# In 21 of 256 Mamba units ScalarE makes the product with B, with time on the partitions, and TensorE turns it into PSUM

## What is computed

```
rn = resid * rsqrt(mean(resid^2) + EPS) * norm_w
skip = rn @ skip_w.T
x_in = rn @ in_w.T
x = silu(conv(x_in))                    # causal, 4 taps, along time
delta = softplus(x @ wd1.T @ wd2.T + wd2_b)
Bm = x @ wB.T ;  Cm = x @ wC.T          # (L, 16) each
def step(h, (d_l, b_l, c_l, x_l)):      # h: (B, E, N)
    h = exp(d_l[:, :, None] * A) * h + (d_l * x_l)[:, :, None] * b_l[:, None, :]
    y_l = einsum('ben,bn->be', h, c_l)
y = (ys + x * W_D) * silu(skip)
return resid + y @ out_w.T
```

## Time and profile before

| | us |
|---|---|
| median of three runs | 1861.87 (1861.37 to 1863.11) |
| the profiled execution, its own time | 1862.27 |
| its span in the trace | 1860.5 |
| the Mamba layer in that span | 0 to about 912 |
| first scan to last scan | about 42 to 905 |
| granted TensorE clock, mean over the span | 0.976 |

### The profile page before, as it was taken

One profiled execution on the slowest core, in us unless ns is written; L12 is line 12 of the kernel. 1 busy time (PEld: TensorE's weight loads), 2 busy tenths in 40 slices (PEclk: granted clock), 3 DMA queues, 4 the chain that ended last, 5 costly groups with the idle time before them and its releaser, 6 DMA issues. The chain is left out here.

```text
span 1860.5 us, 26382 instructions
## 1 busy us (share of the span) xinstructions
PE 1704.0 (92%) x9245; PEld 1340.8 (72%) x9245; DVE 1474.0 (79%) x2310; ACT 1074.6 (58%) x1871; POOL 1100.2 (59%) x711
## 2 busy tenths in 40 slices
PE   6887989899898989966889999999999899999999
PEld 2455656565666666655778888888888788888888
DVE  4889999999999999999787777776345676666664
ACT  5867787878778787777534444443443444444442
POOL 2879999999999999999852222220454432222220
PEclk9899999999999999978999999999999999999999
DMA  6223333232333233344011111121000011111111
GB/s 200 83 77 98 102 98 102 87 113 92 107 96 99 93 107 99 96 150 140 7 35 35 35 35 35 35 57 23 7 0 0 1 46 45 44 38 46 46 46 46
DMA packets 113918, 125.63 MB, mean 68 GB/s; under 512 B 18816, under 2 KB 66048, under 8 KB 113664
## 3 DMA queue, kind: packets, MB, share of 16 engines
q1 hardware_dynamic: 113792, 124.03, 22.9%
HBM read 95.14 MB, written 4.72 MB: 54 GB/s over the span
## 5 line engine op out<-in xcount | busy, mean ns | idle before, releaser
L383 POOL TENSOR_TENSOR m_U<-m_U,m_C 128x1024 f32<-128x1024 f32 x255 | 601.0, 2369 | 26.0 <-DVE m_U L890 15.8
L525 PEld LDWEIGHTS m_y<-ident,m_U 128*128 128x128 f32 x2048 | 249.9, 147 | 117.8 <-issue 71.1
L890 DVE TENSOR_TENSOR_SCAN m_U<-m_dA,m_carry,m_U 128x512 f32<-128x512 f32 x256 | 310.5, 1262 | 4.9 <-ACT m_dA L758 4.5
L525 PE MATMUL m_y<-ident,m_U 128*128 128x128 f32 x2048 | 282.5, 284 | 29.4 <-POOL m_U L383 29.2
L890 DVE TENSOR_TENSOR_SCAN m_U<-m_dA,m_U 128x512 f32<-128x512 f32 x256 | 295.9, 1203 | 11.8 <-ACT m_dA L758 8.4
L758 ACT ACTIVATE m_dA<-high,m_negA 128x512 f32<-128x512 f32 x256 | 172.4, 685 | 74.2 <-DVE m_U L890 73.8
L758 ACT ACTIVATE m_dA<-even,m_negA 128x512 f32<-128x512 f32 x256 | 170.8, 684 | 56.6 <-DVE m_U L890 55.5
L1164 POOL TENSOR_TENSOR SW<-g_Rt 128x512 f32<-128x512 f32 x32 | 40.3, 1290 | 251.5 <-DMA g_CT<-SW 236.7
L1164 POOL TENSOR_TENSOR SW<-f_Rt 128x512 f32<-128x512 f32 x32 | 41.0, 1312 | 226.3 <-DMA f_CT<-SW 225.1
L506 PE MATMUL m_psB<-m_stack,m_pick 128*128 128x512 f32 x196 | 100.7, 514 | 34.1 <-DVE m_U L873 33.9
L873 DVE TENSOR_TENSOR m_U<-even,m_psB 128x1024 f32<-128x1024 f32 x100 | 119.6, 1196 | 12.0 <-PE m_psB L506 11.8
(11 more groups left out here) (389 smaller groups left out, 4414.6 us busy)
## 6 DMA issues: line engine op xcount, KB each, us to landing
m_C<-bc_rows SPq DMA_DIRECT2D x256, 256.0 KB, 3.2
m_B<-bc_rows SPq DMA_DIRECT2D x60, 256.0 KB, 3.5
f_CT<-SW SPq DMA_DIRECT2D x128, 64.0 KB, 2.1
g_CT<-SW SPq DMA_DIRECT2D x128, 64.0 KB, 2.1
even<-in_ffn_w SPq DMA_DIRECT2D x16, 256.0 KB, 5.2
f_z_raw<-f_turned_z SPq DMA_DIRECT2D x112, 32.0 KB, 1.9
g_z_raw<-g_turned_z SPq DMA_DIRECT2D x112, 32.0 KB, 1.9
out<-res SPq DMA_DIRECT2D x7, 512.0 KB, 2.8
```

What stands on the lines that cost most here:

```text
L383: pool.tensor_tensor(u, u, C[:, M % C_RING, :].unsqueeze(1).to_broadcast([P, PE_E, CHUNK]), ALU.mult).then_inc(hc_ready, 1)
L525: last = nc.tensor.matmul(y[:, t, j * P:(j + 1) * P], U[:, M % U_RING, j, t * P:(t + 1) * P], ident[:, :], start=False, stop=n == N - 1, i ...
L890: nc.vector.tensor_tensor_scan(u, dA[:, s % A_RING, :], u, carry[:, e, n:n + 1] if q else 0.0, ALU.mult, ALU.add).then_inc(scan_done, 1)
```

## The change

In chunks 1 to 7 three units in each (5, 10 and 19 of the chunk) are **turned**: 21 in all. For such a unit neither `spread_B` nor VectorE's or GpSimd's product is made. In their place:

- ScalarE holds `dxT` (dx with time on the partitions, four tiles of 128 steps) and `BT` (B the same way). `product(M)` multiplies, with B as the scale of each partition, in four instructions of 128x256 into the unit's place of the U ring, two steps ahead.
- TensorE's `turn_product(M + 1, j)` turns the four 128x128 blocks of each channel block into the PSUM bank of the dA ring that the decay would have had: j = 0 ahead of the parts of its step, j = 1 behind them.
- ScalarE writes the two decays of that unit to an SBUF tile `dAT`, and the scan takes the decay from there and the product from PSUM.
- For `dxT` and `BT` each chunk has new parts: `tr0` to `tr3` and `bt`, four transposes on TensorE and one copy on ScalarE each. `tr2` stands at unit 6, `tr3` at 9 (ScalarE: 10), `tr0` at 28, `tr1` and `bt` at 31.
- The 60 units of GpSimd stay 60, at other places: (3, 7, 12, 14) in the first half of chunks 1 to 7, (6, 9, 12, 15) in the second half of odd chunks, (6, 10, 13) in that of even ones. So VectorE makes 175 products in place of 196.
- To make room in SBUF the ring of C goes from eight tiles to three and that of B from two to one, loaded two units ahead. Two copies of feed-forward weights move from units 21 and 26 of the last chunk to 26 and 28.

The diff, cut to its core:

```diff
-    U_RING, C_RING, A_RING, B_RING = 6, 8, 3, 2
-    ON_POOL, AHEAD = ((3, 7, 10, 14), (4, 9, 14), (3, 7, 11, 14), (3, 6, 10, 14)), 3
+    U_RING, C_RING, A_RING = 6, 3, 3
+    ON_POOL, AHEAD, B_AHEAD = [((3, 7, 10, 14), (4, 9, 14))] + [((3, 7, 12, 14), (6, 9, 12, 15)), ((3, 7, 12, 14), (6, 10, 13))] * 4, 3, 2
+    TURNED, TURN_AHEAD = [((), ())] + [((5, 10), (3,))] * (CHUNKS - 1), 2
...
-                 5: ("cv1", "back3"), 6: ("cv1+",), 7: ("in2",), 8: ("cv2",), 9: ("cv2+",), 10: ("in3",),
+                 5: ("cv1", "back3"), 6: ("cv1+", "tr2"), 7: ("in2",), 8: ("cv2",), 9: ("cv2+", "tr3"), 10: ("in3",),
...
-                 27: ("out1",), 28: ("out1+",), 29: ("back0",), 30: ("back1",),
+                 27: ("out1",), 28: ("out1+", "tr0"), 29: ("back0",), 30: ("back1",), 31: ("tr1", "bt"),
...
-                if M in pool_units:
-                    i = BEFORE[M]
-                    need(sp, pool_mult, i - B_RING + 1)
-                    sp.dma_start(B[:, i % B_RING, :],
-                                 bc_rows[q, n:n + 1, :].to_broadcast([P, CHUNK])).then_inc(B_ready[i % B_RING], 16)
+                if M + B_AHEAD in pool_units:
+                    n_b = place(M + B_AHEAD)[3]
+                    assert n_b >= B_AHEAD
+                    need(sp, pool_mult, POOL_BEFORE[M + B_AHEAD])
+                    sp.dma_start(B[:, :], bc_rows[q, n_b:n_b + 1, :].to_broadcast([P, CHUNK])).then_inc(B_ready, 16)
...
+            def turn_product(M, j):
+
+                s = PE_E * M + j
+                pe.wait_ge(UT_ready, TURNED_BEFORE[M] + 1)
+                pe.wait_ge(scan_done, s - A_RING + 1)
+                for t in range(TILES):
+                    last = nc.tensor.transpose(dA[:, s % A_RING, t * P:(t + 1) * P],
+                                               U[:, M % U_RING, j, t * P:(t + 1) * P], ident[:, :])
+                last.then_inc(UT_turned, 1)
...
-                if M + 2 < ALL_UNITS and M + 2 not in pool_units:
+                if M + 2 in dve_units:
                     spread_B(M + 2)
+                if M + 1 in turned_units:
+                    turn_product(M + 1, 0)
                 for name, k in parts_of(PE_AT, M):
                     part(name, k)
+                if M + 1 in turned_units:
+                    turn_product(M + 1, 1)
...
-                nc.scalar.activation(dA[:, s % A_RING, :], delta[q][:, e, :], ACT.Exp,
+                to = dAT[:, s % PE_E, :] if s // PE_E in turned_units else dA[:, s % A_RING, :]
+                nc.scalar.activation(to, delta[q][:, e, :], ACT.Exp,
                                      scale=negA[:, e, n:n + 1]).then_inc(dA_ready, 1)
+
+            def product(M):
+
+                c, q, p, n = place(M)
+                for e in range(PE_E * p, PE_E * (p + 1)):
+                    wait_freed(act, f"tr{e}", c)
+                wait_freed(act, "bt", c)
+                act.wait_ge(nsum_done, M - U_RING + 1)
+                for t in range(TILES):
+                    last = nc.scalar.activation(U[:, M % U_RING, :, t * P:(t + 1) * P], dxT[:, pair(p), t, :], ACT.Copy,
+                                                scale=BT[:, t, n:n + 1])
+                last.then_inc(UT_ready, 1)
...
+                if M + TURN_AHEAD in turned_units:
+                    product(M + TURN_AHEAD)
...
+                decay, product = dA[:, s % A_RING, :], u
+                if M in turned_units:
+                    dve.wait_ge(UT_turned, PE_E * TURNED_BEFORE[M] + j + 1)
+                    decay, product = dAT[:, j, :], dA[:, s % A_RING, :]
```

More of the change, by code:

```diff
@@ L151, in mamba @@
         B_full, rows_ready, rows_out = sem("B_full"), sem("rows_ready"), sem("rows_out")
[L152 removed]
+        B_ready, pool_mult = sem("B_ready"), sem("pool_mult")
+        UT_ready, UT_turned = sem("UT_ready"), sem("UT_turned")
         C_ready = [sem(f"C_ready{i}") for i in range(C_RING)]
@@ L191, in mamba @@
         BEHIND = {"out0": -1, "out0+": -1, "out1": -1, "out1+": -1, "gate1": -1, "back2": -1, "back3": -1,
-                  "gate0": 0, "back0": 0, "back1": 0, "silu_g": 0, "sum": 2, "square": 2, "factors": 2, "norm": 2, "double": 2}
+                  "gate0": 0, "tr2": 0, "tr3": 0, "back0": 0, "back1": 0, "silu_g": 0, "sum": 2, "square": 2, "factors": 2, "norm": 2, "double": 2}
         ASKED = dict(enumerate((4, 1, 5, 0), CHUNKS))
@@ L199, in parts_of @@
             late = [(name, k) for slot, name, k in at["late"] if c == CHUNKS - 1 and slot == i]
-            chunks = [(name, k) for name, k in chunks if 0 <= k < CHUNKS and (name, k) != ("back1", CHUNKS - 1)]
+            chunks = [(name, k) for name, k in chunks if 0 <= k < CHUNKS and (name, k) != ("back1", CHUNKS - 1)
+                      and (k > 0 or name[:2] != "tr")]
             return chunks + late
@@ L239, in place, with before @@
             return c, c % 2, i // N, i % N
-        pool_units = [M for M in range(ALL_UNITS) if M % N in ON_POOL[M // N % (2 * PASSES)]]
-        BEFORE = [len([m for m in pool_units if m < M]) for M in range(ALL_UNITS)]
+        pool_units = [M for M in range(ALL_UNITS) if M % N in ON_POOL[M // UNITS][M // N % PASSES]]
+        turned_units = [M for M in range(ALL_UNITS) if M % N in TURNED[M // UNITS][M // N % PASSES]]
+        dve_units = [M for M in range(ALL_UNITS) if M not in pool_units and M not in turned_units]
+        def before(units):
+            return [len([m for m in units if m < M]) for M in range(ALL_UNITS + 1)]
+        POOL_BEFORE, TURNED_BEFORE, DVE_BEFORE = before(pool_units), before(turned_units), before(dve_units)
         def pair(p):
@@ L443, in part @@
                     last = mm(take(name, k), [(rnT[:, d, t:t + P], skw[:, d, :]) for d in range(KD)])
+                elif name[:2] == "tr":
+                    e = int(name[2])
+                    pe.wait_ge(dx_ready, KE * k + e + 1)
+                    out = take(name, k)
+                    for t in range(TILES):
+                        last = nc.tensor.transpose(out[:, t * P:(t + 1) * P], dx[q][:, e, t * P:(t + 1) * P],
+                                                   ident[:, :])
+                elif name == "bt":
+                    pe.wait_ge(rows_ready, k + 1)
+                    out = take(name, k)
+                    for t in range(TILES):
+                        last = nc.tensor.transpose(out[:, t * 2 * N:(t + 1) * 2 * N], rows[:, t * P:(t + 1) * P],
+                                                   ident[0:2 * N, 0:2 * N])
                 elif name[:2] == "cv":
@@ L889, in scan @@
                 dve.wait_ge(dA_ready, s + 1)
-                nc.vector.tensor_tensor_scan(u, dA[:, s % A_RING, :], u, carry[:, e, n:n + 1] if q else 0.0,
+                nc.vector.tensor_tensor_scan(u, decay, product, carry[:, e, n:n + 1] if q else 0.0,
                                              ALU.mult, ALU.add).then_inc(scan_done, 1)
@@ L908, in _ @@
             for M in range(ALL_UNITS):
-                if M + 1 < ALL_UNITS and M + 1 not in pool_units:
+                if M + 1 in dve_units:
                     mult(M + 1)
```

47 lines of the change are left out of this document (29 added, 18 removed), and 4 rows, old and new, of the table ACT_AT.

## The result

The changed kernel takes **1878.16 us** (median; 1876.83 to 1883.15), the kernel before 1861.91 (1860.7 to 1863.11): ratio 1.0091, 95% interval 1.0081 to 1.0101. It is 16.2 us slower. The forecast was 1860.6, the range ended at 1870: the prediction was wrong, by size and by sign. The profiled execution took 1877.32 us (span 1875.6).

The account below looks back on a forecast made before the run. The prediction took GpSimd to bound even chunks and VectorE odd ones. Chunks 1 to 4 gave +1.4, 5 and 6 -2.0, 7 -0.7: -1.3 on the profiled 1862.3, with the median 0.4 lower: 1860.6 us; range 1849 to 1870.

Parts of the forecast that it names:

- What bounds the kernel: Whole stretch: GpSimd sets even chunks, VectorE odd ones; a lighter VectorE can give at most GpSimd's 19.7 us of waits.
- VectorE, ScalarE, TensorE, DMA as single terms: VectorE 23.3 us less; per chunk ScalarE 81.8 to 89.4, TensorE 96.0 to 99.8 of 106; C's loads hidden.
- First half of an odd chunk: Walk from unit 5 to unit 10: waits sum to 2.3 us against 2 x 1.11 saved, net +0.1; wait bounds 1.0 and 3.5.
- Second half: Odd chunk: GpSimd's fourth product adds 2.33 us, less 0.6 won and waits of 0.7 and 0.4 swallowed, net +0.6.
- Even chunks: Set by GpSimd, with 0.4 us of waits in chunk 2; VectorE's lead grows there but cannot be used.
- Slower, TensorE paces the first half: TensorE's 22.8 us in steps 3 to 9 exceed VectorE's 21.0; 1.4 us in each of six chunks, 1870 us; chance 0.18.
- Faster: VectorE's lead from even chunks lasts through odd first halves, GpSimd pacing throughout; 1849 to 1856 us, middle 1853; chance 0.36.
- C's lateness: Rows of C land later than 4.7 us, at chunk starts or in chunk 7; 8 us more, 1870; chance 0.07.
- transposes that don't overlap: TensorE's 44 transposes cost 0.272 us each, 12.0 a chunk, filling it to 107 of 106; 1869 us; chance 0.02.

Follow-up runs that it names:

- r16: Changed kernel with each block of a turned unit turned twice into the same slot, 8 transposes where there were 4: 1893.53 us.
- r10: Changed kernel with dx's third quarter turned in step 7, behind the next input product, instead of step 6: 1874.44 us.
- r17: Kernel before with the changed kernel's smaller rings, B's fetch and later weight copies; no turned unit, no parts, old places of GpSimd's products: 1860.55 us.
- r4: Changed kernel with only the second halves' unit turned and GpSimd's new places there; first halves as in the kernel before: 1868.99 us.
- r9: Changed kernel with GpSimd's products of second halves at 5, 8, 11, 14 and 5, 9, 12: 1873.25 us.
- r2: Kernel before with the changed kernel's rings, B's fetch and the parts that turn dx and B, their results unused; no turned unit: 1866.82 us.
- r5: Changed kernel with its places of GpSimd's products and its parts, but no turned unit; VectorE makes those 21 products: 1874.29 us.
- r13: Changed kernel with dx's third quarter turned in step 7 and GpSimd's second-half products at 5, 8, 11, 14 and 5, 9, 12: 1867.39 us.
- r3: Changed kernel with only units 5 and 10 of first halves turned; second halves as in the kernel before: 1881.62 us.

## Why the prediction was wrong, point by point

**What bounds the kernel.** The windows were read for busy shares over whole chunks, where TensorE has 96 of 106 us. That was the wrong grain: in the 44.8 us behind the gate of chunk 3 it was busy for 42.9. Behind the first gate TensorE starts late, since it waits for `y` to be free, and works off the delay while VectorE runs on. In that stretch the kernel before let it wait 1.9 us for VectorE, and that was all it had to give. The change asks for four groups of transposes (1.76), the two parts `tr2` and `tr3` (0.88), the waits for bank and product (0.87 + 0.17), less two spreads (0.64): 3.0 us. That is 1.1 more than there was; the half became 1.7 longer. This account is worked out from the rows, not tested as a whole; r16 and r10 test its terms.

**VectorE, ScalarE, TensorE, DMA as single terms: right.** Minus 21 products. `product` took 1.69 us (predicted 1.7), four transposes 0.44 us on the path (r16: 5.2 us for 48 more transposes, 109 ns each; the Trainium skill's 275 ns, on the page the prediction names, is their duration and not what one adds: the trace of the kernel before has 272 ns), and C's smaller ring cost nothing (r17).

**First half of an odd chunk: this is the step that failed.** The walk from unit 5 to unit 10 was nearly right in its sizes as far as it went. Predicted waits 0.3, 0.7, 0.4, 0.6, 0.3, measured 0.27, 0.72, 0.51, 0.73, 0.62, and unit 5 ended 10.5 us behind its gate (predicted 10.4). Two of the five agree by luck. The first was predicted for the first scan of unit 5, behind `product(5)`; it stood at unit 4, whose decays come behind the silu, and unit 5's first scan waited for nothing. And the wait for the row of unit 8 was put down to `tr2`, but that spread stands ahead of `tr2` in step 6, and r10, which moves `tr2`, leaves it at 0.51. But the walk stopped at unit 10 and took what stood there for the whole price. The lateness went on: 0.87 us at unit 15 where the kernel before had 0.3, since the silu of x now stands behind a part that waits for TensorE (0.44 us). The sum is 3.7, not 2.3, or 3.4 more than before; and I also let each wait cost its bracket alone, while an instruction that waits no longer overlaps the one before it by 0.1 us (six waits where there was one). 3.4 + 0.5 - 2.2 = 1.7: the predicted +0.1 was +1.7, and the upper bound of 3.5 us of waits was passed.

**Second half.** Predicted +0.6, measured +0.9 (r4, and the changed kernel). The mechanism was another one than named: not that GpSimd's fourth product fills its waits, but that VectorE stops 1.6 us at unit 31, whose product stands last in GpSimd's order. r9 moves the places and gets 0.3 back in chunk 3, 1.0 in chunk 4. That the size came near is luck.

**Even chunks: the second failure.** They were written off as GpSimd's, so that nothing there could cost. Chunk 4 took 2.6 us more, as much as an odd one. GpSimd, which before waited 0.4 us in chunk 2, now waits 2.1 in chunk 4. The parts alone cost 1.1 us in an even first half (r2: 53.3 for 52.2): the term that I had hidden in TensorE's room.

**The rivals.** "Slower, TensorE paces the first half" (0.18) was what happened, at its place, by its condition (waits of 3.7 against 2.2 saved, 1.5 above, where it needed 1) and in even chunks through GpSimd, as it said. Its price, 1.4 us in each of six chunks, was too small: measured about 2.6 in seven, of which r2 gives 0.85 to the parts, r5 1.1 to the places and the rest, 0.65, to the turned units net of what they save. "Faster" failed on the same point: with TensorE setting the pace, VectorE's saved time is only a wait. C's lateness and transposes that don't overlap are excluded by r17 and r16. Of the 0.7 us by which the two repairs miss their sum in r13's pair, 0.6 goes with the clock: its halves of chunks 1 and 2 with the second half of chunk 4 make 213.5, and the first half of chunk 4 takes 53.3 us where that of chunk 2 takes 52.85; in the last 14 us ahead of them TensorE's granted clock was 0.75 and 0.88. The changed kernel shows the same between chunk 2 (54.8) and chunk 4 (53.9). This is read from traces, not tested.

## What to carry to other kernels

An engine at 90% over a chunk (96 of 106 us) stood at 96% in the stretch where it works off a delay (42.9 of 44.8), and that left no room: count its waits for the engine that you relieve in just that stretch, for they are all it can take over. When several engines hand a ring of buffers round in program order, walk a change on until the waits stop, and price a wait that is shifted into the next part as a wait. Move work onto the path of a third engine only in place of the work that binds: here the same turned unit cost nothing where it took GpSimd's product in the second half, and two of them cost 1.4 to 1.7 us a half net where they took VectorE's in the first (r3 against r2).
